# A sixth GpSimd product with C in units 2 and 4 of each batch of a Mamba + FFN block

## The reference

```
proj = xn Win^T ; hs, gate = two halves of 1024 channels
hs = silu(conv4(hs) + bconv) ; dt_in, B, C = hs Wx^T ; dt = softplus(dt_in Wdt^T + bdt)
h[t] = exp(-exp(A_log[d,n]) * dt[t]) * h[t-1] + dt[t] * B[t,n] * hs[t]
y[t] = sum over n of h[t] * C[t,n]   (float32)
out  = ((y + hs * D) * silu(gate)) Wout^T
```

## Time and profile before

| what | us |
|---|---|
| three runs of the kernel | 1082.05, 1083.62, 1084.32 (median 1083.62) |
| the profiled execution | 1084.43 |
| its span, first to last instruction | 1082.6 |
| DVE busy | 1018.7 |
| POOL busy | 893.2 |
| ACT busy | 829.2 |
| stage B, first scan to last | 222.1 to 1067.5 |

### The profile page before, as it was taken

How to read it: one execution, slowest core, us unless ns; L and a number is a source line. 1 busy time by engine, 2 the same in 40 slices (tenths; PEclk the granted TensorE clock), 3 DMA queues, 4 the chain that set the end, 5 groups by cost and what they waited for, 6 DMA issues and landing times.

```text
span 1082.6 us, 14656 instructions
## 1 busy us (share of the span) xinstructions
PE 926.4 (86%) x4318; PEld 574.6 (53%) x4328; DVE 1018.7 (94%) x1214; ACT 829.2 (77%) x1154; POOL 893.2 (83%) x496
## 2 busy tenths in 40 slices
PE   3978899868778997898889979987998799879998
PEld 2746566435555555455545545555555455545554
DVE  6979898599999999999999999999999999999996
ACT  3777877678889865888897668988966689889662
POOL 4344535699999899989998999899989989998993
PEclk9999999888888998999989988999899899989999
DMA  7687778992111218432212193421212923212101
GB/s 280 186 272 236 291 220 320 353 371 107 53 59 40 87 47 272 179 125 73 78 37 88 40 320 118 136 78 59 71 57 71 345 87 102 78 59 78 40 0 39
DMA packets 53157, 150.24 MB, mean 139 GB/s; under 512 B 5728, under 2 KB 14048, under 8 KB 50016
## 3 DMA queue, kind: packets, MB, share of 16 engines
q1 hardware_dynamic: 53088, 149.41, 39.5%
HBM read 111.37 MB, written 38.01 MB: 138 GB/s over the span
## 4 chain that ended last, share of the span: by engine, by line
DVE 36%; issue 29%; ACT 18%; PE 10%; POOL 5%; DVEq 1%; DMA 1%; POOLq 0%
DVE da L1100 14%; DVE prod L1075 10%; DVE hp L1100 8%; ACT da L994 5%; ACT gate_bf L972 3%; PE yT L1226 3%; POOL dt_du L371 3%; ACT L973 2%; ACT L972 2%; DVE y L1083 2%; ACT L983 2%; ACT L982 2%; POOL hs_lo L366 2%; PE mm L1175 1%; DVE gate_bf L1113 1%
## 5 line engine op out<-in xcount | busy, mean ns | idle before, releaser
L994 ACT ACTIVATE da<-unit,neg_a 128x512 f32<-128x512 f32 x512 | 339.8, 684 | 162.6 <-DVE prod L1075 159.6
L833 POOL TENSOR_TENSOR dbu<-unit,b_head 128x1024 f32<-128x1024 f32 x192 | 449.8, 2370 | 0.0
L1100 DVE TENSOR_TENSOR_SCAN da<-da,dbu 128x512 f32<-128x512 f32 x352 | 416.9, 1214 | 1.2
L1226 PE MATMUL yT<-ident,prod 128*128 128x128 f32 x1408 | 232.8, 296 | 97.7 <-DVE prod L1075 97.1
L1226 PEld LDWEIGHTS yT<-ident,prod 128*128 128x128 f32 x1408 | 176.7, 151 | 225.6 <-DVE prod L1075 175.1
L1063 POOL TENSOR_TENSOR hp<-hp,c_head 128x512 f32<-128x512 f32 x128 | 163.6, 1278 | 58.0 <-DVE gate_bf L1116 53.4
L1100 DVE TENSOR_TENSOR_SCAN hp<-da,dbu 128x512 f32<-128x512 f32 x160 | 193.0, 1206 | 9.5 <-ACT da L994 9.5
L1075 DVE TENSOR_TENSOR prod<-da,c_head 128x512 f32<-128x512 f32 x256 | 170.4, 666 | 0.0
L1175 PE MATMUL mm<-xn_b,w_sb 128*128 128x512 fp8e4 x512 | 150.0, 428 | 3.8 <-ACT gate_bf L1009 2.7
L833 POOL TENSOR_TENSOR dbu<-unit,b_all 128x1024 f32<-128x1024 f32 x64 | 151.4, 2366 | 0.0
L1187 PE MATMUL mm<-xnT_b,wgate 128*128 128x512 f32 x256 | 128.9, 601 | 2.0 <-ACT gate_bf L1009 1.7
(11 more groups left out here) (118 smaller groups left out, 1281.7 us busy)
## 6 DMA issues: line engine op xcount, KB each, us to landing
unit<-unit_d SPq DMA_DIRECT2D x32, 768.0 KB, 4.3
unit_d<-dt_du SPq DMA_DIRECT2D x32, 512.0 KB, 2.7
wf<-in_wffn SPq DMA_DIRECT2D x12, 1024.0 KB, 6.6
c_head<-bc_d SPq DMA_DIRECT2D x24, 512.0 KB, 4.1
b_head<-bc_d SPq DMA_DIRECT2D x18, 512.0 KB, 4.9
unit_d<-hs SPq DMA_DIRECT2D x32, 256.0 KB, 6.4
w_sb<-w_d SPq DMA_DIRECT2D x64, 128.0 KB, 3.9
wgate<-in_win_gate SPq DMA_DIRECT2D x32, 256.0 KB, 2.7
```

The source lines that it names most:

```text
L833: return nc.gpsimd.tensor_tensor(dbu[:, n % DBUS:n % DBUS + NS, :], twice, b_all[n // NS], ALU.mult)
L994: nc.scalar.activation(da[n % SLOTS][:, :], unit[:, k % 2, 0, :], ACT.Exp, scale=neg_a[:, k, n:n + 1]).then_inc(da_ready, 1)
L1100: nc.vector.tensor_tensor_scan(state, da[n % SLOTS][:, :], dbu[:, n % DBUS, :], 0.0, ALU.mult, ALU.add).then_inc(scanned, 1)
L1226: ins = nc.tensor.matmul(yT[k % 2][:, t * P:(t + 1) * P], product[:, t * P:(t + 1) * P], ident[:, :], start=False, stop=last, is_transpose ...
```

## The change

In units 2 and 4 of each batch POOL multiplies six states with C, 1, 4, 6, 8, 10 and 12, where it multiplied five, 1, 4, 7, 9 and 12. DVE multiplies ten there and not eleven. The other six units keep their five. The table `FOUR`, which nothing used, is gone. There are 42 pooled states in a batch (before 40) and 86 own ones (before 88); no other line is changed.

```diff
-FIVE, FOUR = (1, 4, 7, 9, 12), (1, 4, 8, 12)
-POOLED = (FIVE,) * KU
+SIX, FIVE = (1, 4, 6, 8, 10, 12), (1, 4, 7, 9, 12)
+POOLED = (FIVE, FIVE, SIX, FIVE, SIX, FIVE, FIVE, FIVE)
```

## The result

The changed kernel takes 1087.71 us (median of 13 runs, 1085.47 to 1089.0), the kernel before 1083.25 us in the same comparison (13 runs). The ratio is 1.0040, 95% interval 1.0031 to 1.0048: 3.4 to 5.2 us slower. The forecast was 1086.9 in a range of 1084.0 to 1089.6. The profiled execution took 1088.33 us (span 1086.5), 3.9 more than the one of before. One run of the kernel before and one of experiment 10 took 1800 us and aren't counted; the second is the one that was profiled, and of its profile, in which PE is slow throughout, only durations on DVE and POOL are read.

What follows compares the result with a forecast made beforehand. POOL's dbu tiles, ready only 0.25 to 0.42 us ahead of the last scans, were taken to decide. Losses of 4 x 0.61 + 4 x 0.22 = 3.3 us on the median 1083.62 gave 1086.9, range 1084.0 to 1089.6.

Steps and rivals of the forecast that it cites:

- the handoff: From POOL's dbu end to DVE's waiting scan: taken as 0.05 us, with 0 and 0.18 as ends.
- Margins decide, and DVE's saving isn't in the formula: Units 2 and 4: each late scan loses 1.23 plus 0.05 less its old margin; DVE's saved 0.59 is used up at scan 12.
- All dbu tiles from 10 on come 1.23 later: Units 2 and 4: one more POOL product stands before each of dbu 10, 12, 14 and 0, ending them 1.23 us later.
- Scans 12, 14 and 0 behind by 0.16, 0.86 and 1.00: Unit 2 and the next scan 0: DVE waits for dbu and starts these scans that many us behind the old times.
- ACT's wait absorbs 0.39 of it behind unit 2: Scan 1 of the next unit already waits 0.39 us for ACT, so 1.00 less 0.39 leaves 0.61 lost.
- After unit 4, 0.22, with ACT's chain just below: Scan 1 after unit 4: 1.03 late less ACT's 0.81 wait loses 0.22 us, just above ACT's own slip of 0.16 to 0.18.
- gate_bf meets the end of dbu 6, 0.08, and loses nothing: Following unit: gate_bf would start 0.08 us before dbu 6 ends; cost taken as nothing, at most 0.6 us in all.
- The delay doesn't pass on: POOL still waits for the clamp, by about 0.6 and 1.0 us less, so the unit after starts as it does now.
- The rings cost nothing, "distance of 5": Rings hp and prod keep distances of 5 and at least 6 tiles against a reader following within a few states: nothing.
- A busier POOL slows no scan or product: Scan stage: DVE's product takes 0.66 us beside idle or busy POOL; the skill's shared-port rule would add up to 9.8 us.
- The upper end of the range: 1089.6 us: the forecast with 0.18 handoffs, given as 1088.5, and run scatter of 1.1.
- (d): Rival: gate_bf held by dbu 6 with a restart, handoffs of 0.18: 4.9 us more, or 7.3 and 1091; chance 0.08.

Runs made afterwards that it cites:

- experiment 10: Changed kernel with the six pooled states of units 2 and 4 set to 1, 2, 4, 7, 9 and 12, the sixth product ahead of the clamp: 1088.96 us, ratio 1.0035.
- experiment 1: Kernel before plus one POOL product into an unread spare tile in units 2 and 4, DVE keeping its eleven products: 1086.93 us, ratio 1.0023.
- experiment 2: Changed kernel with POOL multiplying only 8 of the 512 tokens of state 6 in units 2 and 4: 1078.69 us, ratio 0.9951.
- experiment 12: Kernel before with ACT's six copies out of the ffn banks in units 0 to 3 one state earlier (9 to 14): 1076.65 us, ratio 0.9921.
- experiment 9: Changed kernel without POOL's wait for the clamp ahead of the product of state 4: 1144.46 us, ratio 1.0574.
- experiment 3: Kernel before with six pooled states in unit 2 of each batch only, five-tile ring hp: 1093.12 us, ratio 1.0077.
- experiment 4: Kernel before with six pooled states in unit 4 of each batch only, five-tile ring hp: 1090.61 us, ratio 1.0056.
- experiment 8: Kernel before with six pooled states in units 1 to 4 of each batch, twice the change: 1093.05 us, ratio 1.0076.
- experiment 5: Kernel before with six pooled states in unit 2 only and the ring hp of six tiles, not five: 1086.5 us, ratio 1.0024.
- experiment 6: Kernel before with six pooled states in unit 4 only and the ring hp of six tiles, not five: 1084.82 us, ratio 1.0013.

## Why the prediction was right

The mechanism was the one forecast: late dbu tiles, each by POOL's product plus the handoff less the margin. The size was close: 3.3 us forecast, 3.7 in the two traces' units, 3.4 to 5.2 by the runs, so that 3.3 lies just under what the runs allow. Two of its terms came out right partly by luck, as said below. By its steps:

- *Margins decide, and DVE's saving isn't in the formula.* Shown by experiments 1 and 2: POOL's product without the saving costs the same 3.3 us, and the saving without the product gains 4.1.
- *All dbu tiles from 10 on come 1.23 later.* Measured against scan 5: dbu 14/15 ended 13.22 us after it, now 14.49, dbu 0/1 16.78 and now 18.03, 1.27 and 1.25 later.
- *Scans 12, 14 and 0 behind by 0.16, 0.86 and 1.00.* Measured against scan 5: 11.03 for 10.80, 14.59 for 13.64, 18.13 for 17.06: 0.23, 0.95 and 1.07. Every one is 0.07 to 0.09 more. About half of that is the handoff, taken as 0.05 by the nearest rows and measured as 0.09 to 0.10; the rest is dbu tiles that are up to 0.04 later than 1.23.
- *ACT's wait absorbs 0.39 of it behind unit 2.* It absorbed 0.46: scan 1 is 0.61 later (19.86 for 19.25), just as forecast, though scan 0 is 1.07 later. The idle time of 0.39 counts from the end of product 15, but the next instruction of DVE starts some 0.08 before that end (503.20 against 502.61+0.66 = 503.27) when it needn't wait. A recorded wait is that much smaller than the slack from start to start. The two errors, 0.07 and 0.07, cancelled, which is luck; experiment 12, which took away the wait, shows the true slack of 0.48.
- *After unit 4, 0.22, with ACT's chain just below.* 0.23 to 0.25 in three of the four, but by another path than the forecast's: ACT's chain was last after all. Its slip follows scan 12, and was 0.23 rather than 0.16. DVE alone would have reached scan 1 at 19.86 from scan 5, as in unit 2 where it waits for nothing, and that is 0.18 late (19.68 in unit 4 before). The odd unit of batch 1 shows ACT's path by itself: its scan 12 is 0.36 later than elsewhere, its scans 14 and 0 are not, and its scan 1 is again 0.35 later.
- *gate_bf meets the end of dbu 6, 0.08, and loses nothing.* In unit 3 of batch 1 dbu 6 ends at 520.11+2.37 = 522.48, gate_bf starts at 522.38: 0.10 of overlap, and it takes 0.95 as in the earlier trace rows. A larger one would have cost: at 0.92 it lost 0.79 (experiment 10), at 0.85 it lost 0.72 (experiment 9). So of this instruction's overlap all but some 0.13 is lost. The other kind of instruction in the earlier trace rows got 0.22 free (1.30 less 1.08).
- *The delay doesn't pass on.* All other units kept their length, and POOL's wait for the clamp in unit 3 shrank from 2.39 to 1.75, by 0.64 (forecast 0.6), and in the units 5 of batches 0, 2 and 3 by 1.0, as forecast.
- *The rings cost nothing, "distance of 5".* The result held and the reason was wrong. With 42 states and 5 tiles the distance falls to 2 at a batch change; it was covered by 2.2 us. With 41 states it would have been 1 and have cost 5 to 7 us (experiments 3 and 4), which would have put the forecast outside its range.
- *A busier POOL slows no scan or product.* Held: they kept their 1.2 and 0.66 us, so the up to 9.8 us more of the shared port are out. The two engines do hold each other up elsewhere: experiment 9 made the two bf16 instructions 2.7 and 3.8 times as long. That is not what made this change slower.
- *The upper end of the range.* The 1088.5 is called the forecast with handoffs of 0.18, but that gives 1083.6+3.3+1.0 = 1088.0; the other 0.6 is the meeting with gate_bf of (d).

The forecast had nothing for the odd 0.36 us in unit 4 of batch 1. They come from scan 12, which starts 0.44 after the end of its dbu, where all others take 0.09 to 0.10, and they explain 0.36 of the 0.4 by which the traces exceed the forecast. The traces of the experiments tell more about it. Experiment 8 has the same 0.44 to 0.45 four times, at scan 10 of unit 1 in batch 0, unit 2 in batch 1, unit 3 in batch 2 and unit 4 in batch 3, nine units apart each. The first of them (its dbu ends at 260.00+2.35 = 262.35):

```profile
260.00 2.35 POOL L833 TENSOR_TENSOR dbu<-unit,b_head 128x1024 f32<-128x1024 f32 x1
262.80 1.22 DVE L1100 TENSOR_TENSOR_SCAN hp<-da,dbu 128x512 f32<-128x512 f32 x1 [0.36 <-issue]
```

If one counts every record of DVE in the trace from 0, its waits for semaphores included, these four are number 581, 1093, 1605 and 2117. The odd scan here is number 1221, also with a ring of six tiles and in experiment 2. Scan 0 behind unit 5 of batch 0 in experiments 3 to 6, 0.45 to 0.46 after its dbu, is number 837. All of these differ by multiples of 128. At every other scan of these profiles, apart from those that the ring holds at the batch changes, the start follows within 0.06 us from the dbu, the da and the instruction before it. So at some fixed places of DVE's program, a multiple of 128 records apart, a scan starts no earlier than some 0.44 us after its dbu, and this shows only where the dbu comes just in time. What DVE does there stays open.

The median's 4.5 is inside what the runs' interval allows, and so is the traces' 3.7; before scan 5 of the first unit alone the profiled executions differ from the one of before by 1.0 us more to 2.1 less, so a single pair of executions can't settle the rest.

## What to carry to other kernels

A share of 83% busy says nothing about room: list, for each thing that the engine hands over, how long before its use it is done, and compare the smallest of these with the work to be added. What the relieved engine saves counts only if the loaded one still delivers in time; then the consumer is late by the added duration plus the handoff less the smallest margin, whatever was saved, and the loss is that less what a later wait of the consumer absorbs. And when a change alters how many entries a ring sees per round, work out the reuse distance at the wrap, where count modulo size sets it.

## What the runs showed of the hardware

- DVE starts 0.09 to 0.10 us after the recorded end of the POOL instruction that it waits for, against 0.04 after ACT's and 0.13 after PE's modelled end (438.25 to 438.38).
- At some places of DVE's program, a multiple of 128 of its records apart, the scan starts 0.44 us after the end of the POOL instruction that it waits for, and not 0.09.
- The bf16 product of two SBUF tensors and its clamp on DVE and POOL's instructions exclude each other, with some 0.13 us of overlap free: 0.10 of overlap cost the product nothing, 0.92 cost it 0.79. POOL is held too: in experiment 9 the dbu that starts at 254.39, just ahead of the product's release, takes 3.06 us and not 2.35. The Trainium skill, page "SBUF — State Buffer", section on the two separate sides, describes the port pair as an exclusive lock held for the whole instruction; these rows agree.
